# Chunks 1 to 3 of a transformer layer take their layer norm in the weights and the evictions, under a new list of steps

## What is computed

```
n1  = layernorm(x)                            # over the 256 columns, eps 1e-5
qkv = n1 @ Wqkv;  rates from n1 @ [Wlr, Wm, Ws] (+ biases bm, bs)   # 768 + 20 columns
for chunk in 4 chunks of 128 tokens, for each of 4 x 4 (batch, head) states:
    out   = (silu(q W0) * (q W2)) W1          # read the states
    dW0, dW1, dW2 = gradients of the chunk + decayed momentum
    5 Newton-Schulz steps:  A = X X';  B = b A + c A A;  X = a X + B X   # 64 x 64 matrices
    W = renormed(W + X)
y   = rmsnorm(out) * silu(...) + windowed attention(q, k, v)
x1  = x + layernorm(y @ Wo)
out = x1 + layernorm(gelu(layernorm(x1) @ proj1 + b1) @ proj2 + b2)
```

## Time and profile before

| | us |
|---|---|
| median of 3 runs (lowest, highest) | 382.04 (381.73, 382.21) |
| the profiled execution: span from first to last instruction | 380.1 |
| PE busy | 371.0 |
| DVE, ACT, POOL busy | 257.6, 213.3, 193.9 |
| PE idle before its first instruction / after its last to the end | 1.0 / 5.1 |

### The profile page before, as it was taken

How to read it: one execution, slowest core, us unless ns; L and a number is a source line. 1 busy time by engine, 2 the same in 40 slices (tenths; PEclk the granted TensorE clock), 3 DMA queues, 4 the chain that set the end, 5 groups by cost and what they waited for, 6 DMA issues and landing times.

```text
span 380.1 us, 15979 instructions
## 1 busy us (share of the span) xinstructions
PE 371.0 (98%) x6760; PEld 295.4 (78%) x6760; DVE 257.6 (68%) x682; ACT 213.3 (56%) x432; POOL 193.9 (51%) x290
## 2 busy tenths in 40 slices
...
DMA packets 12677, 10.84 MB, mean 29 GB/s; under 512 B 4544, under 2 KB 12096, under 8 KB 12608
## 3 DMA queue, kind: packets, MB, share of 16 engines
...
...
## 4 chain that ended last, share of the span: by engine, by line
PE 86%; DVE 4%; SPq 3%; issue 2%; POOL 2%; ACT 1%; DMA 1%; POOLq 0%; DVEq 0%; ACTq 0%
PE pair L782 15%; PE pair L793 15%; PE pair L713 6%; PE pair L701 6%; PE pair L691 6%; PE pair L559 6%; PE pair L682 5%; PE pair L591 4%; PE pair L763 3%; PE pair L732 3%; PE pair L568 3%; PE pair L748 3%; PE pair L662 2%; PE pair L739 2%; PE pair L629 1%
## 5 line engine op out<-in xcount | busy, mean ns | idle before, releaser
L782 PE MATMUL pair<-xn2T,p1T 128*128 128x512 f32 (+1 forms) x160 | 59.1, 512 | 0.0
L793 PE MATMUL pair<-p2T,h 128*128 128x256 f32 x256 | 57.0, 379 | 0.0
L793 PEld LDWEIGHTS pair<-p2T,h 128*128 128x128 f32 x256 | 48.0, 190 | 6.4 <-issue 0.2
L1424 POOL TENSOR_SCALAR var<-mv 128x1 f32<-128x1 f32 (+1 forms) x55 | 13.1, 239 | 67.1 <-DVE mv L1382 37.4
L1034 ACT ACTIVATE h<-pair,b 128x512 f32<-128x512 f32 (+1 forms) x40 | 23.9, 602 | 36.0 <-PE pair L782 35.9
L782 PEld LDWEIGHTS pair<-xn2T,p1T 128*128 128x128 f32 x160 | 28.7, 190 | 17.1 <-issue 14.8
L1419 POOL TENSOR_TENSOR nq<-ssq,half 128x8 f32<-128x8 f32 (+1 forms) x16 | 24.2, 1513 | 27.5 <-DVE ssq L1141 27.5
L1056 DVE SCALAR_TENSOR_TENSOR A<-pair,eye 128x512 f32<-128x512 f32 x45 | 28.7, 683 | 13.2 <-PE pair L691 13.1
L1419 POOL TENSOR_TENSOR rstd<-var,neg_half 128x1 f32<-128x1 f32 (+1 forms) x55 | 33.5, 609 | 4.6
L1056 DVE SCALAR_TENSOR_TENSOR B<-pair,eye 128x512 f32<-128x512 f32 x45 | 28.9, 684 | 10.2 <-PE pair L701 10.0
L559 PE MATMUL pair<-wqkv,xnT 128*128 128x512 f32 x64 | 31.5, 627 | 0.6 <-ACT xnT L816 0.6
...
## 6 DMA issues: line engine op xcount, KB each, us to landing
x_in<-in_L_attn_x_dram SPq DMA_DIRECT2D x16, 128.0 KB, 2.5
x<-in_L_attn_x_dram SPq DMA_DIRECT2D x16, 128.0 KB, 2.1
out_dram<-rows_a SPq DMA_DIRECT2D x16, 128.0 KB, 1.7
...
wo<-in_L_attn_Wo_dram SPq DMA_DIRECT2D x1, 256.0 KB, 7.7
...
```

Of the source, the lines that this page charges most:

```text
L782: mm_ = pe.matmul(ps[:, at], p1T[:, k, n * P:(n + 1) * P], xn2T[:, k, at], start=(k == 0), stop=(k == KC - 1))
L793: mm_ = pe.matmul(ps[:, 0:DIM], h[:, n, b * P:(b + 1) * P], p2T[:, n, :], start=(n == 0), stop=(n == HC - 1))
```

## The change

Layer norm of chunks 1 to 3. The mean over the rows is taken out of the weights: with M the mean over the 256 inputs of each of the 788 columns, `(x - m) @ W` equals `x @ (W - M)`. `CS.0` (DVE) sums the rows of the transposed weights; `CM.0` (SP) sends the 788 means to a DRAM tensor in pieces of one element, and loads them back broadcast to 128 partitions (`cm_wide`); `CW.0` (POOL) subtracts them from `wqkv` after the last product of chunk 0. `rstd1` is multiplied in at the evictions of `QK` and `VV`. `xnT` of chunks 1 to 3 is loaded from a transposed copy of x that the host lays out (`XD`), so `LNX` and `XT` of these chunks are gone.

Loads. The states come as the kernel holds them, W and its transposes (1.5 MB in place of 192 KB), so `WI.0` on DVE and `WX.0` are gone; biases and scales come in one packed array; the first load of `wqkv` holds the 512 columns of QK alone. SP's later DMAs now stand in the list too (`XA`, `XI`, `XD`, `F2N`).

Smaller ones: after `XT.0.0` PE runs three products of ones with 64 columns; the last row group's epsilon is added by DVE.

```diff
-            def XT_(bank, c, b=None):
+            def XT_(bank, c, b):
...
-                pe.wait_ge(*S["xn"](c, 1))
                 for k in range(KC):
-                    ps = take(bank[k], "xnT", c, k + 1)
-                    for b in range(BATCH):
-                        mm_ = pe.transpose(ps[:, b * P:(b + 1) * P], xn[:, b, k * P:(k + 1) * P], ident[:, :])
-                    mm_.then_inc(S["xT_ps"].sem, 1)
+                    mm_ = pe.transpose(ps[:, k * P:(k + 1) * P], xn[:, b, k * P:(k + 1) * P], ident[:, :])
+                mm_.then_inc(S["first_xT"].sem, 1)
+                if b == 0:
+                    for n in range(3):
+                        pe.matmul(BANK[7][:, 0:64], ones[:, :], ones[:, 0:64], start=True, stop=True)
...
+            def x_ready(c, b):
+                if c == 0:
+                    pe.wait_ge(*S["first_xnT"](0, b + 1))
+                    return
+                pe.wait_ge(*S["xT_in"](c, 16))
+                if c == 1:
+                    pe.wait_ge(*S["centred"](0, 1))
...
+                act.activation(raw[:, b, 0:512], BANK[bank[0]], ACT.Copy, scale=rstd1[:, c % 2, b:b + 1]).then_inc(S["qk_raw"].sem, 1)
...
+            def CS(c):
+                dve.wait_ge(ld_rows, 32)
+                dve.tensor_reduce(col_sum[:, 0:6], w_rows[:, 0:6, :], AX.X, ALU.add)
+                dve.tensor_reduce(col_sum[0:SMALL, 6:7], w_rows[0:SMALL, 6:7, :], AX.X, ALU.add).then_inc(S["col_sum"].sem, 1)
...
+            def CM(c):
+                sp.wait_ge(*S["col_mean"](0, 1))
+                sp.dma_start(cm_sent[0:6 * P].rearrange("(m p) -> p m", p=P), col_mean[:, 0:6], allow_slow_non_contiguous=True)\
+                    .then_inc(S["cm_sent"].sem, 16)
...
+                sp.wait_ge(*S["cm_sent"](0, 32))
+                sp.dma_start(cm_wide[:, :], cm_sent.partition_broadcast(P)).then_inc(S["cm_wide"].sem, 16)
...
+            def CW(c):
+                pool.wait_ge(*S["cm_wide"](0, 16))
+                pool.wait_ge(*S["qk_ps"](0, BATCH))
+                pool.wait_ge(*S["v_ps"](0, BATCH))
+                for k in range(KC):
+                    last = tt(wqkv[:, k, :], wqkv[:, k, :], cm_wide[:, :], ALU.subtract)
+                last.then_inc(S["centred"].sem, 1)
...
+                if c == 0:
+                    act.wait_ge(*S["centred"](0, 1))
...
+                if ends(c, b):
+                    dve.wait_ge(*S["f2_mv"](c, b + 1))
+                    dve.tensor_scalar(var4[:, b:b + 1], mv4[:, b, 1:2], LN_EPS, None, ALU.add).then_inc(S["f2_var"].sem, 1)
```

More of the change, by code:

```diff
@@ L102 @@
     first_stats=4, first_mv=4, first_var=4, first_rstd=4, first_xn=4, first_xT=4, first_xnT=4,
-    ln1_stats=1, ln1_mv=1, ln1_var=1, ln1_rstd=1, xn=1, xT_ps=2, xnT=2,
+    ln1_stats=1, ln1_mv=1, ln1_var=1, ln1_rstd=1, xT_in=16, col_sum=1, col_mean=1, cm_sent=32, cm_wide=16, centred=1,
     lr_neg=1, lr_exp=1, lr_log=1, lr=1, ms_tanh=1, ms=1, mm_ps=1, mm=1, decayed=3,
@@ L136 @@
 ORDER = steps("""
[L137 to L141, removed]
@@ L147 @@
[L147 to L151, removed]
@@ L157 @@
[L157 to L161, removed]
@@ L182 @@
-    F2N.2.1 F2N.2.2 F2N.2.3 F1.3.6.0 NT.3.3 F1.3.7.0 L2N.3.3 F1.3.0.1 F1.3.1.1 F1.3.2.1 F1.3.3.1 F1.3.4.1 F1.3.5.1
-    F1.3.6.1 F1.3.7.1 F2.3.0 F2.3.1 F2N.3.0 F2.3.2 F2N.3.1 F2.3.3 F2N.3.2 F2N.3.3
+    LN1.0.0 CO.0 LNX.0.0 LN1.0.1 EY.0 LNX.0.1 LN1.0.2 LN1.0.3 XT.0.0 QK.0.0 CM.0 XD.1 LNX.0.2 LNX.0.3 XT.0.1
+    VV.0.0 XT.0.2 SI.0.0 VV.0.1 NQ.0.0 CS.0 QK.0.1 NR.0.0 XT.0.3 VV.0.2 SI.0.1 NQ.0.1 WI.0 LN1.1 QK.0.2 SI.0.2
+    VV.0.3 NQ.0.2 QK.0.3 SM.0 SI.0.3 TR.0.0 NR.0.1 NQ.0.3 TR.0.1 TR.0.2 TR.0.3 TR.0.4 NR.0.2 MS.0 TR.0.5 S.0.0
@@ L302, in layer_kernel @@
         var1 = sb("var1", BATCH)
-        rstd1 = sb("rstd1", BATCH)
+        rstd1 = sb("rstd1", 2, BATCH)
+        col_sum = sb("col_sum", 7)
+        col_mean = sb("col_mean", 7)
         xnT = sb("xnT", KC, BATCH * P)
@@ L376, in layer_kernel @@
         dsig, dgba = gms, dxh
-        w_in = share(X, 0, 3, 2, HD)
+        w_rows = share(h, 0, 7, DIM)
+        cm_wide = share(h, 2048, 3 * DIM + SMALL)
         sg, dhbm = share(X, 0, 2, 8, HD), share(XT, 512, 2, 8, HD)
@@ L434, in mask_of, with ends @@
             return mask[:, seen(c):2 * P] if slot(c) else mask[:, P:3 * P]
+        def ends(c, b):
+            return c == CHUNKS - 1 and b == BATCH - 1
         def learns(c):
@@ L474, in _ @@
[L474 to L482 removed]
+            sp.dma_start(wqkv[:, :, 512:], Wall[:, 512:].rearrange("(k p) n -> p k n", p=P)).then_inc(ld_v, 16)
@@ L1126, in VV @@
                     dve.wait_ge(*S["pv_ps"](c - 1, b + 1))
-                dve.tensor_copy(v_rows[:, slot(c), b, :], BANK[bank[0]][:, 0:DIM])
+                if c:
+                    dve.wait_ge(*S["ln1_rstd"](c, 1))
+                    dve.tensor_scalar(v_rows[:, slot(c), b, :], BANK[bank[0]][:, 0:DIM], rstd1[:, c % 2, b:b + 1], None, ALU.mult)
+                else:
+                    dve.tensor_copy(v_rows[:, slot(c), b, :], BANK[bank[0]][:, 0:DIM])
                 if b == 0:
```

305 lines of the change are left out of this document (160 added, 145 removed).

## The result

The changed kernel takes 387.25 us (median of 4 runs, 386.99 to 387.77), the kernel before 382.12 in 4 runs on the same chip: ratio 1.0133, 95% interval 1.0118 to 1.0147. It is 5.1 us slower. Forecast were 380.4 (377.3 to 383.9), most likely faster: wrong in sign and outside the range. The profiled execution has a span of 385.5, before 380.1.

The account below looks back on a forecast made before the run. PE, busy 98%, was taken as the bound, with POOL taking over before DW.0.0. Terms -1.9 - 0.5 + 3.1 - 2.0 - 0.3 = -1.6 on the span of 380.1 gave 378.5, plus 1.9 around it 380.4 (range 377.3 to 383.9).

Parts of the forecast that it names:

- I take in time: Chunk 0: cm_wide lands between 25.4 and 33, taken as before POOL needs it at CW (27.8 or up to 1.8 later).
- rival A: Chunk 0: the means come late, so POOL stands at CW and PE's VV.1.0 waits; slower, 384.2; chance 0.12.
- my own formula: Chunk 0, from cm_wide's landing: CW takes 3.1, the rest up to the last KL 10.5; landing at 31.5 puts DW.0.0 at 45.1.
- rival D: Start of chunk 0: QK.0.0 takes 1.72, not 3.55, so POOL starts up to 1.7 earlier; DW.0.0 gains 2.1; chance 0.20.
- XT.2, XT.3, ten visits, one QK for one VV: PE behind DW.0.0: two transposes gone -1.9, ten more visits to small steps at 0.31 each +3.1, step swap +0.7.
- DW.0.0: End of chunk 0's start: POOL's chain to the last KL binds, 41.4 to 43.2 if the head keeps pace; -0.5 taken.
- Waits: Between PE's steps: fewer tight Newton-Schulz pairs (20 for 29) against more table loads; -2.0, bounds -5 to +3.
- Tail: End of kernel: last epsilon shorter on DVE than 0.22 on POOL, row group before finished ahead; -0.3 (0 to -0.5).
- B: The new list brings no fewer waits; table loads and one-by-one steps give back 2; +2.4, 384.4; chance 0.15.
- C: Visits to small steps are free when spread, the mode change hiding in existing waits; 377.3; chance 0.12.

Follow-up runs that it names:

- e1: Changed kernel with the loads of p1T, p2T and wo issued behind the broadcast of the means instead of ahead of the two writes; ratio to before 1.0246.
- e14: Changed kernel with the first write in 128 pieces of 24 bytes, p1T, p2T and wo loaded behind the broadcast, xnT ahead of it; ratio to before 0.9993.
- e3: Changed kernel with nine products ident x p1T put on PE right ahead of VV.1.0's wait for the centred weights; ratio to before 1.0287.
- e11: Changed kernel with four products ident x p1T put on PE right ahead of VV.1.0's wait for the centred weights; ratio to before 1.0173.
- e9: Changed kernel with the means made by PE products of ones, no DRAM trip, and DVE subtracting from PSUM in place of CW; ratio to before 1.0075.
- e2: Changed kernel with the centring of the weights left out (sums, writes, broadcast, subtraction and their waits); ratio to before 0.9998.
- e5: Changed kernel with transposed weights laid out so the first write of means is 128 pieces of 24 bytes, not 768 of 4; ratio to before 1.0034.
- e8: Kernel before with 13 full-array steps moved into runs of small steps beside them, 13 visits more, no other edit; ratio to before 1.0176.
- e12: Kernel before with only the change's three products of ones added behind XT.0.0; ratio to before 0.9991.
- e13: The edits of e9 under the list of the kernel before, with VV.1.0 and VV.1.1 at their old place ahead of TR.0.8; ratio to before 0.9999.

## Why the prediction was wrong

**The step that failed is "I take in time"**, with rival A beside it at 0.12. Forecast was `cm_wide` between 25.4 and 33, and "in time" (by 27.8, or up to 1.8 later) was taken from it; it landed at 32.0, inside my own bounds, and the chance of the upper part was set too low. The bounds themselves are not the sum of their terms: 17 + 3.6 + 3.8 is 24.4, and 17 + 7.7 + 7.7 is 32.4. The argument against A was that both trips would have to be as slow as `wo`. But the writes were priced by a load of 4 KB in single elements (3.6). The two writes with their wait took 9.5 with no weights ahead (e1), of which 8.1 lie behind the last packet, so the nearest row was the wrong one: it was a read. That DVE was done 1.4 early did not help.

**What A costs was under-sized too.** By my own formula a landing at 32.0 gives DW.0.0 at 45.6 (3.1 and 10.5 behind it); it came at 47.6. CW took 3.65 for 3.1, which puts POOL's last KL at 46.1, and for the rest the clock was missing: I had weighed only a faster QK.0.0 at the start (rival D) and never asked what a wait of PE does to it. Between e14 and the changed kernel the account closes: VV.1.0 3.12 later, and 2.72 more from there to DW.0.0, of which VV.1.0 and QK.1.0 at a clock of 0.50 are 1.97 - 1.03 and 3.55 - 1.81, 2.7. Together 5.8 of DW.0.0, 5.4 of the span. The clock of 0.50 goes with PE's idle time, not with the load of `xnT` or POOL's work: both of these were there in e3 and e11 too, where PE was kept at work and the granted clock stayed at 1.00. Where the wait is not 3.7 but the clock alone is mended (e11), 1.4 of the 2.7 come back before y sets DW.0.0.

**The rest of the sum, by e14**, where A is gone. Its ratio would be 381.9 on the first chip; forecast 380.4.
- XT.2, XT.3, ten visits, one QK for one VV: -1.9 + 3.1 + 0.7 = +1.9 forecast behind DW.0.0, +1.7 by the table. Right.
- DW.0.0: 41.3 forecast (41.8 - 0.5), 41.7 measured. The size is right, the reason is not. POOL's chain went as summed: in e14 it idles 0.34 in all from the first power on, and its last KL ends at 41.1 (forecast 41.4). But it did not bind: DW.0.0 came 0.6 after it without a wait, and e9 without CW on POOL gained 0.5 only. PE's own steps set it, with stops of 0.78 and 1.40 for ACT on the way, and in e2, e5 and e9 DVE's y. That the sizes agree is luck.
- Waits: -2.0 forecast, -0.6 measured (6.8 to 6.2). The largest miss beside A. Part of it is the gaps on "issue": behind DW.0.0 they are 0.3 in the kernel before and 1.1 in e14, and without them the waits went from 6.5 to 5.1, -1.4. The rest was over-sized: fewer tight pairs in a list are not waits saved one for one.
- Tail: -0.3 forecast, -0.3 in the changed kernel and -0.4 in e14.
- A misreading without effect: the small step alone at 280.04 is an NB, not an NA.

**The rivals.** A happened. B (the list gives back 2 of waits) did not happen, nor did my 2 less: the new list has 0.6 (e14) to 1.1 (changed kernel) less. C is refuted by e8. D (0.20: QK.0.0 at the 1.72 of a later QK step in place of 3.55, so that POOL starts up to 1.7 earlier and DW.0.0 gains 2.1 for 0.5) was an estimate from that row. The faster QK.0.0 is in the trace after (1.79 to the next step, 3.55 before), but e12 shows that it brings nothing (ratio 0.9991, 0.9982 to 1.0001), e2 and e11 that it can fail to come with the three products (3.45 and 3.52), and e8 that it comes without them too (four instructions in 1.95).

**What stays open.** What the 768 pieces do in the 8 us between their last packet and their landing, and whether their number or their size is at fault; and why PE's gaps on "issue" stand in one kernel and not in the next. No kernel beat the one before: e2, e12, e13 and e14 equal it.
